# The reciprocal root of the layer norms: ScalarE's square root against a bit guess and three Newton turns on VectorE

## The reference, cut to what matters

```python
def _layernorm(x, axis=-1, eps=1e-05):
    m = jnp.mean(x, axis=axis, keepdims=True)
    v = jnp.var(x, axis=axis, keepdims=True)
    return (x - m) / jnp.sqrt(v + eps)

x = x + 0.5 * _L0_ffn_ref(_layernorm(x), ...)    # ffn0a: silu(gate) * up, hidden 768
x = x + _L0_attn_ref(_layernorm(x), ...)         # qkv0, att0, out0
x = x + 0.5 * _L0_ffn_ref(_layernorm(x), ...)    # ffn0b
x = x + 0.5 * _L1_ffn_ref(_layernorm(x), ...)    # ffn1a: gelu, hidden 1024
x = x + _L1_attn_ref(_layernorm(x), ...)         # qkv1 (with rotation), att1, out1
x = x + 0.5 * _L1_ffn_ref(_layernorm(x), ...)    # ffn1b
```

## Time and profile before

| | us |
|---|---|
| median of 3 runs | 2133.86 |
| lowest and highest of them | 2127.05 and 2134.82 |
| the profiled execution, its own time | 2129.82 |
| its span in the profile | 2128.0 |
| PE busy (share) | 2000.9 (94%) |
| DVE busy (share) | 1635.1 (77%) |
| ACT busy (share) | 1345.7 (63%) |
| POOL busy (share) | 511.2 (24%) |

### The profile page before, as it was taken

How to read it: one execution, slowest core, us unless ns; L and a number is a source line. 1 busy time by engine, 2 the same in 40 slices (tenths; PEclk the granted TensorE clock), 3 DMA queues, 4 the chain that set the end, 5 groups by cost and what they waited for, 6 DMA issues and landing times. The chain is left out here.

```text
span 2128.0 us, 43648 instructions
## 1 busy us (share of the span) xinstructions
PE 2000.9 (94%) x16326; PEld 1245.0 (59%) x16326; DVE 1635.1 (77%) x2925; ACT 1345.7 (63%) x2591; POOL 511.2 (24%) x572
## 2 busy tenths in 40 slices
PE   5998989999999999997998999988999999989999
PEld 4887733333333333336887888864444444448888
DVE  6776699999999999927776544789999999927333
ACT  4444348888888888882444455554777777753554
POOL 2000142121141241141100311585321212222110
PEclk9999969999999999999999999997999999999999
DMA  4002943235346335123001000395555565320000
GB/s 150 1 0 108 319 70 58 47 65 95 69 72 98 79 66 90 38 58 105 1 0 65 1 0 0 104 275 129 92 113 103 107 118 102 82 58 30 20 20 30
DMA packets 124371, 161.60 MB, mean 76 GB/s; under 512 B 54668, under 2 KB 77900, under 8 KB 124180
## 3 DMA queue, kind: packets, MB, share of 16 engines
q1 hardware_dynamic: 101156, 112.32, 25.0%
q0 software_dynamic: 16256, 37.82, 6.7%
q10 hardware_dynamic: 6768, 8.91, 1.3%
HBM read 94.02 MB, written 63.70 MB: 74 GB/s over the span
## 5 line engine op out<-in xcount | busy, mean ns | idle before, releaser
L1630 ACT ACTIVATE att_probs<-att_s_exp 128x512 f32<-128x512 f32 (+3 forms) x1792 | 883.3, 551 | 202.3 <-PE att_s_exp L1528 164.8
L1665 DVE TENSOR_REDUCE maxes<-att_s_max 128x2 f32<-128x1024 f32 x640 | 771.4, 1222 | 33.6 <-PE att_s_max L1486 28.7
L1553 PE MATMUL att_o_ps<-att_probs,att_v_st 128*32 128x256 f32 (+2 forms) x6400 | 514.2, 393 | 10.2 <-ACT att_o_sb L1607 9.1
L1553 PEld LDWEIGHTS att_o_ps<-att_probs,att_v_st 128*32 128x32 f32 x6400 | 127.1, 108 | 253.7 <-issue 137.1
L1659 DVE CUSTOM_DVE_ANT_0 att_s_max<-att_s_max,mask_q 128x384 f32<-128x384 f32 (+3 forms) x512 | 235.3, 522 | 24.0 <-PE att_s_max L1486 21.7
L1528 PE MATMUL att_s_exp<-first_q,first_k 64*128 64x512 f32 (+3 forms) x672 | 178.1, 471 | 1.4 <-DMA first_q<-att_m_parts 0.8
L1486 PE MATMUL att_s_max<-first_k,first_q 62*128 62x512 f32 (+3 forms) x672 | 146.4, 433 | 23.0 <-DVE maxes L1665 11.6
L1528 PE MATMUL att_s_exp<-w_lo,w_hi 64*128 64x512 f32 x640 | 164.5, 497 | 1.5 <-DMA w_lo<-att_m_parts 1.5
L1749 POOL TENSOR_TENSOR att_m_parts<-m_turned,att_zeros 32x128 fp32r<-32x128 f32 x64 | 29.0, 452 | 496.0 <-ACT m_turned L1596 359.1
L1528 PEld LDWEIGHTS att_s_exp<-w_lo,w_hi 64*128 64x128 f32 x640 | 63.1, 183 | 134.2 <-ACT att_probs L1630 123.6
L1528 PEld LDWEIGHTS att_s_exp<-first_q,first_k 64*128 64x128 f32 x672 | 78.7, 189 | 100.7 <-ACT att_probs L1630 88.0
(11 more groups left out here) (327 smaller groups left out, 4375.9 us busy)
## 6 DMA issues: line engine op xcount, KB each, us to landing
attention_rows<-att_o_sb POOLq DMA_DIRECT2D x64, 256.0 KB, 4.6
output_wide<-attention_weights POOLq DMA_DIRECT2D x36, 256.0 KB, 5.6
first_q<-q_parts SPq DMA_DIRECT2D x132, 64.0 KB, 5.2
first_k<-k_parts SPq DMA_DIRECT2D x66, 128.0 KB, 4.5
q_parts<-qkv_parts SPq DMA_DIRECT2D x16, 512.0 KB, 4.4
k_parts<-qkv_parts SPq DMA_DIRECT2D x16, 512.0 KB, 4.3
att_v_raw<-v_rows SPq DMA_DIRECT2D x32, 256.0 KB, 6.1
output_o_t<-attention_rows POOLq DMA_DIRECT2D x16, 512.0 KB, 7.2
```

Source lines behind the costliest of these rows:

```text
L1553: mm = pe.matmul(o_ps[j * VW:(j + 1) * VW, cols], v_st[:, it.par, kt, j, :], probs[:, step % 2, j, cols], start=kt == 0 and opens, stop=st ...
L1630: act.activation(probs[:, step % 2, j, q0:512], s_exp[:, plan.bank[place], q0:512], ACT.Exp, scale=1.0 if causal else 0.25).then_inc(s["ex ...
L1665: v.tensor_reduce(maxes[:, qc, :, pairs, qt - 4 * qc, kc], banks, AX.X, ALU.max).then_inc(s["max_done"], 1)
```

## The change

The change does three things.

1. `norm_root` is gone from all twelve places, and with it every table load for it. `norm_rstd` works on VectorE alone: the bits of the variance shifted right by one and subtracted from a constant give a first guess y, and three turns of y * (1.5 - 0.5 * v * y * y) refine it. That is 2 + 3 x 3 = 11 small chained steps where 5 stood. `norm_variance` keeps its seven instructions.
2. In ffn0a's first chunk all of chunks 4 to 7 are measured by halves beside f = 0 to 3, the variance moves between h and its low part of f = 4, and the root stays after f = 5.
3. In the other feed-forwards' first chunk the variance stays after f = 1, and `norm_rstd` moves from after f = 4 to after f = 2.

```diff
-NORM_STEPS = 6
-RSTD_STEPS = 5
+NORM_STEPS = 7
+ROOT_GUESS = 1597463007.0
+ROOT_TURNS = 3
+RSTD_STEPS = 2 + 3 * ROOT_TURNS
...
-    v.wait_ge(std, 1)
-    chain(v.reciprocal(a, E.std[:, at]))
-    chain(v.tensor_tensor(c, b, a, ALU.mult))
-    chain(v.tensor_tensor(a, c, E.std[:, at], ALU.add))
-    chain(v.tensor_scalar(c, a, 0.5, None, ALU.mult))
-    chain(v.reciprocal(E.rstd[:, at], c))
+    y = E.rstd[:, at]
+    chain(v.tensor_scalar(a.bitcast(I32), b.bitcast(I32), 1, None, ALU.logical_shift_right))
+    chain(v.tensor_scalar(y.bitcast(I32), a.bitcast(I32), -1.0, ROOT_GUESS, ALU.mult, ALU.add))
+    for _ in range(ROOT_TURNS):
+        chain(v.scalar_tensor_tensor(out=c, in0=y, scalar=-0.5, in1=y, op0=ALU.mult, op1=ALU.mult))
+        chain(v.tensor_tensor(c, c, b, ALU.mult))
+        chain(v.scalar_tensor_tensor(out=y, in0=c, scalar=1.5, in1=y, op0=ALU.add, op1=ALU.mult))
...
-def norm_root(act, E, var, std, at):
-    act.wait_ge(var, 1)
-    act.activation(E.std[:, at], E.ln_b[:, at], ACT.Sqrt).then_inc(std, 1)
...
                 act.activation(jobs[i][0][0][:, :, :], split.raw[i][:, :, :], ACT.Copy).then_inc(s["hi"], 1)
-                if i == 0:
-                    norm_root(act, E, s["next_var"], s["next_std"], NEXT)
...
-        unmeasured = range(EARLY_CHUNKS, CHUNKS - 1) if E.x_in else range(0)
-        rest_at = 1 + 2 * bool(E.x_in)
+        unmeasured = range(EARLY_CHUNKS, CHUNKS) if E.x_in else range(0)
+        rest_at = len(unmeasured) or 1
...
                         statistics(v, E, unmeasured[f], range(CT // 2))
+                    if f == rest_at and first and unmeasured:
+                        v.wait_ge(s["ln_step"], 1)
+                        n = norm_variance(v, E, s["ln_step"], REST, 1)
                     v.wait_ge(s["h_hi"], c * F + f + 1)
...
-                        statistics(v, E, unmeasured[f], range(CT // 2, CT))
-                    if f == rest_at and first:
+                        ins = statistics(v, E, unmeasured[f], range(CT // 2, CT))
+                        if f == len(unmeasured) - 1:
+                            ins.then_inc(s["ln_step"], 1)
+                    if f == rest_at and first and not unmeasured:
                         n = rest_variance(v, E, s)
-                    if f == max(4, rest_at + 2) and first:
-                        norm_rstd(v, E, s["ln_step"], s["ln_std"], REST, n)
+                    if f == rest_at + 1 and first:
+                        norm_rstd(v, E, s["ln_step"], REST, n)
```

More of the change, by code:

```diff
@@ L164, with norm_variance @@
 REST_STEPS = 1 + NORM_STEPS + RSTD_STEPS
-def norm_variance(v, E, step, var, at, n=0):
+def norm_variance(v, E, step, at, n=0):
     me, ve, mo, vo = (E.stats[:, at, i] for i in (1, 2, 4, 5))
@@ L182, in norm_variance @@
     chain(v.tensor_scalar(a, b, 1.0 / D, EPS, ALU.mult, ALU.add))
-    v.scalar_tensor_tensor(out=b, in0=c, scalar=0.25, in1=a, op0=ALU.mult, op1=ALU.add).then_inc(var, 1)
-    v.wait_ge(var, 1)
+    chain(v.scalar_tensor_tensor(out=b, in0=c, scalar=0.25, in1=a, op0=ALU.mult, op1=ALU.add))
     chain(v.tensor_tensor(c, me, mo, ALU.add))
@@ L188, in norm_variance, with norm_rstd @@
     return n
-def norm_rstd(v, E, step, std, at, n):
+def norm_rstd(v, E, step, at, n):
     a, b, c = E.ln_a[:, at], E.ln_b[:, at], E.ln_c[:, at]
@@ L327, in load_stage @@
     with ExitStack() as ctx:
-        s = semaphores(nc, E, name, "small", "cast", "hi", "peaks", "peak", "peak_turned", "peak_all", "next_step", "next_var",
-                       "next_std", "ident", "xn_ready", "turned", "hi_ready", "lo_ready")
+        s = semaphores(nc, E, name, "small", "cast", "hi", "peaks", "peak", "peak_turned", "peak_all", "next_step",
+                       "ident", "xn_ready", "turned", "hi_ready", "lo_ready")
         split = Split(nc, E, ctx, name, jobs)
@@ L388, in _ @@
             v.wait_ge(s["next_step"], 1)
-            n = norm_variance(v, E, s["next_step"], s["next_var"], NEXT, 1)
-            norm_rstd(v, E, s["next_step"], s["next_std"], NEXT, n)
+            n = norm_variance(v, E, s["next_step"], NEXT, 1)
+            norm_rstd(v, E, s["next_step"], NEXT, n)
             normalise(v, E, 0, 0, s)
@@ L517, in body @@
                     act.activation(h_parts[0][:, f % HBUFS, :], h[:, f % 2, :], ACT.Copy).then_inc(s["h_hi"], 1)
[L518 to L521, removed]
                     if f == 3 and (follow or not last):
@@ L767, in step @@
                         part_hi(act, E, T, c + 1, 1 - par, s)
-                    if i == QK - 1 and opening(c):
-                        norm_root(act, E, s["ln_var"], s["ln_std"], REST)
             each_tile(act, step)
```

20 lines of the change are left out of this document (8 added, 12 removed).

## The result

| | before | after |
|---|---|---|
| median, us | 2131.43 (8 runs) | 2143.69 (8 runs) |
| lowest and highest | 2123.72, 2134.82 | 2142.03, 2145.44 |
| the profiled execution, its span | 2129.82, 2128.0 | 2143.06, 2141.3 |

The ratio is 1.0065, with a 95% interval of 1.0053 to 1.0077: the change costs 12.3 us by the medians and 14 by the ratio. That is the slow side of the line that the prediction drew at 0.5%, and 1.3 us from its 2145. The 2145 stands on a median of three runs, 2133.86; on the eight runs of this table the same +11.8 us gives 2143.2.

What follows compares the result with a forecast made beforehand. TensorE, busy 94% of the span, was taken as the bound, so only its waits count. Stage terms summed to +10.1 us, one clock fall made +11.8: 2145 us from the three-run median, range 2135 to 2151.

Steps and rivals of the forecast that it cites:

- the line that the prediction drew at 0.5%: Whole kernel: smallest difference measurable, about 0.5% (10.7 us), so slower begins at 2144.5 us; chance of slower 0.46, within 0.52.
- The load stage, +7.3 predicted: Load stage: longer chain makes normalise meet GpSimd's two subtractions, each engine waiting for the other's whole instruction; +7.3 us.
- The rivals with +1.1 and +4.4: Load stage: GpSimd misses normalise (+1.1 us, chance 0.20), or only one of its two subtractions gets ahead (+4.4, 0.13).
- ffn0a's first chunk, -3.3 predicted: ffn0a's first chunk: no table swap and the new order bring h of the next block 3.3 us sooner.
- ffn0b's first chunk, -1.0 predicted: ffn0b's first chunk: h starts 0.45 us sooner, and the chain's earlier place gives more back; between 0.45 and 1.5, taken -1.0 us.
- Last chunks, +3.7 predicted: Last chunks, where TensorE's turn waits for xn behind the longer chain: +1.1 us in ffn0a, +1.5 ffn0b, +1.1 ffn1a.
- ffn0b's +1.5: ffn0b's last chunk: longer chain, with nine two-input steps instead of two, also meets a small GpSimd instruction; +1.1 to +1.8 us.
- qkv0 and qkv1: qkv0 and qkv1: TensorE waits for VectorE work queued behind the norm, so the longer chain costs +1.1 us each.
- out0: out0: TensorE's 5.50 us wait for outputs whose weights come by DMA covers the longer chain; 0.
- out1: out1: TensorE waits 0.67 us for VectorE work queued behind the norm; longer chain costs +1.2 us.
- The clock, +1.7 predicted for one more fall: TensorE's granted clock: longer waits bring none to three more falls to its lower level, 0 to 5.1 us; one taken, +1.7.
- The work terms: Terms for the stages, load to out1, without the clock: their sum was +10.1 us.

Runs made afterwards that it cites:

- pool_behind: Changed kernel, with GpSimd's two weight subtractions in the load stage waiting until xn of chunk 0 is written: 2135.6 us, ratio 1.0031 against the kernel before.
- old_order: Changed kernel with the new root everywhere, but statistics, variance and root back at their old places in the first chunks: 2145.18 us, ratio 1.0077 against the kernel before.

## Why the prediction came out right

**The load stage, +7.3 predicted, +7.5 measured.** Nearly each step stands in the trace as it was worked out: `normalise` at 13.6 (13.5), GpSimd at 13.67 (13.6), its second subtraction at 17.05 (17.1), the gate subtraction at 21.23 (21.1), ffn0a's first matmul at 33.39 (33.2). The alternation, one instruction of VectorE for each of GpSimd's, carried over from ffn1a's. One step differs: the first `normalise` was to go through at 13.5 to 13.8, ahead of GpSimd, and it ended at 17.24. That cost nothing more, because GpSimd's two subtractions stand back to back and the last two `normalise` instructions end the stretch in either order. The rivals with +1.1 and +4.4 are out, and pool_behind shows the first of them as a kernel: +1.4.

**ffn0a's first chunk, -3.3 predicted, -3.4 measured**, and the next late thing was the one named: a wait of 1.41 us for the same h at 58.65, where 51.2 + 7.5 = 58.7 and 1.7 us were expected. The two halves were not priced apart; the runs give 2.0 for the missing swap and 1.4 for the order on top of it. The clock fall of the earlier trace rows is gone too, but it is no further gain: VectorE's queue set the end of this stretch. Stretch, us, PE busy, granted clock, before that DVE, ACT and POOL:

```profile
50.00:55.00 5.00, 5.00 (x31) 4.39 (x31) 3.93 (x14) 1.94 (x4) 0.00 (x0) 1.00 0.02 3
```

**ffn0b's first chunk, -1.0 predicted, -1.9 measured: a mis-sized term.** The first wait shrank by 0.55, as worked out. What the estimate valued at another 0.5 was 1.3: behind it stood three smaller waits (before: 0.26, 0.23 and 0.63 us), all late for the same reason. Of before, then of after:

```profile
1015.49 0.50 PE L134 MATMUL ffn0b_up<-front0b_xt_lo,w_gate_hi 128*128 128x512 f32 x1 [0.26 <-DVE ffn0b_h L608]
1018.78 0.50 PE L134 MATMUL ffn0b_up<-front0b_xt_lo,w_gate_hi 128*128 128x512 f32 x1 [0.23 <-DVE ffn0b_h L608]
1021.53 0.39 PE L136 MATMUL ffn0b_acc<-w_down_hi,ffn0b_h_lo 128*128 128x256 f32 x1 [0.63 <-DVE x L586]
```
```profile
1026.42 0.39 PE L136 MATMUL ffn0b_acc<-w_down_hi,ffn0b_h_lo 128*128 128x256 f32 x1 [0.28 <-DVE x L574]
```

The reason given for it, the new place of the chain, was wrong: old_order gains the same 1.9 us with the old place.

**Last chunks, +3.7 predicted, +2.9 measured.** ffn0b's +1.5 counted nine two-input steps that could meet GpSimd. One step was long, as before:

```profile
1135.02 2.20 DVE L205 SCALAR_TENSOR_TENSOR front0b_ln_c<-ln_rstd 128x8 f32<-128x8 f32 x1
1137.25 0.17 DVE L206 TENSOR_TENSOR front0b_ln_c<-front0b_ln_c,front0b_ln_b 128x8 f32<-128x8 f32 x1
1137.45 0.25 DVE L207 SCALAR_TENSOR_TENSOR ln_rstd<-front0b_ln_c,ln_rstd 128x8 f32<-128x8 f32 x1
```

More steps were no more collisions here: one step in eleven was long. **qkv0 and qkv1** cost 0.9 and 1.0 for 1.1, and **out0** nothing, as predicted. **out1** cost 1.1 for 1.2, but not at the wait named alone: that one grew by 0.74, and the other 0.4 came with the new wait at 1934.64, for x, which VectorE also writes behind the root.

**The clock, +1.7 predicted for one more fall.** The falls moved more than they grew in number. After the longer turn wait in ffn1a the transposes took 1.97 instead of 1.09 us (the shift goes up by 1.4 behind the wait), in ffn0a the stretch behind the turn is now slow (+1.6), and attention 0 got 2.9 back. Of after, three stretches (behind the turn in ffn0a, in att0, behind the turn in ffn1a):

```profile
174.00:180.00 6.00, 6.00 (x26) 5.05 (x25) 3.65 (x8) 2.77 (x6) 0.00 (x0) 0.72 0.00 0
```
```profile
255.00:320.00 65.00, 53.57 (x309) 27.72 (x307) 56.51 (x58) 23.01 (x41) 26.05 (x26) 0.76 0.54 132
```
```profile
1330.00:1336.00 6.00, 3.92 (x16) 3.50 (x17) 3.81 (x13) 0.00 (x0) 0.00 (x0) 0.72 0.01 3
```

Before, the same matmuls of the first ran at 1.00, and 255 to 320 stood at 0.71. The rest line of the table, +2.1, holds all of this. It comes from one execution each, and which wait brings a fall was not tested.

**What the prediction lacked** is the place of the tile: +3.1 us of steady drift, a term it had at nothing. The work terms were 2.0 us too high and hid most of it, so the total is right partly by luck. It leaned on the same line as the result: with the tile kept the ratio is 1.0055 with an interval from 1.0037, so still near even between the two sides; without it it is 1.0065, all of its interval beyond.

## What to carry to other kernels

Before you free one engine, ask what its earlier end releases: here ScalarE was done 0.5 us sooner and VectorE 1.2 us later, which closed a gap of 0.35 us between `normalise` and GpSimd's 3.4 us instructions, and one place of twelve made two thirds of the loss. Each of the two moves is larger than the gap; no run made one without the other. Make such a change place by place: the same root, with the new order, wins where a table swap stands in a full queue (the first chunks of ffn0a and ffn0b, ratio 0.9978), and loses 0.8 to 1.1 us wherever TensorE waits for the chain. And when a change drops or adds a tile, keep the addresses fixed in one run of the comparison; a shift of 128 bytes went with 0.1 to 0.25% here, of which only the 0.25% stands clear of the intervals.

## What the runs showed of the hardware

The time of a matmul depended on where its tiles lie in SBUF: 392 to 393 ns against 396 to 397 for one of three groups of 128x512 in ffn1b, 280 against 281 to 282 for 128x256, with the same instructions, by 128 bytes up or down and not by 256. What in the place does it is open. And VectorE, although its first `normalise` instruction began 0.05 us ahead of GpSimd's, didn't get it through first: the four of them, 0.35 us each alone, lasted 6.3 us longer, about the two of GpSimd's together (6.9). Which of the two engines went first could not be read from starts as near as these.
